# Routing steps of two mixture-of-experts layers moved to other places in a four-stage kernel

## The reference

```python
x = _layernorm(x + _L0_attn_ref(x, ...))   # gathered convolution, 8 heads, 32 taps
x = _layernorm(x + _L0_ffn_ref(x, ...))    # 8 experts, 2 chosen a token, GELU, hidden 512
x = _layernorm(x + _L1_attn_ref(x, ...))   # softmax attention, 16 heads of 8 channels
x = _layernorm(x + _L1_ffn_ref(x, ...))    # 8 experts, 2 chosen a token, gated SiLU, hidden 256
...
logits = xn @ gate_w_moe + gate_b_moe      # first FFN; the second has no bias and no inner norm
tw, ti = jax.lax.top_k(logits, K)
tw = jax.nn.softmax(tw, axis=-1)
```

## Time and profile before

| | us |
|---|---|
| three timed runs | 812.55, 816.96, 818.23; median 816.96 |
| the profiled execution, its own time | 811.2 |
| span from its first to its last instruction | 809.4 |

### The profile page before, as it was taken

The page is one execution under the profiler, slowest core; times in us unless marked ns, Lnnn a source line. Parts: engine busy times, 40 slices in busy tenths (PEclk is TensorE's granted clock), DMA queues, the critical chain, the costliest instruction groups (busy, mean ns, idle before and its releaser), DMA issues. The chain is left out here.

```text
span 809.4 us, 14477 instructions
## 1 busy us (share of the span) xinstructions
PE 530.4 (66%) x5186; PEld 439.2 (54%) x5186; DVE 531.9 (66%) x1210; ACT 413.3 (51%) x909; POOL 204.9 (25%) x195
## 2 busy tenths in 40 slices
PE   5367567575666379999832578888868803878730
PEld 4256566464566278899832444454544503878720
DVE  2989989999996225575624477888875304654734
ACT  5576766778852254477633436767654202333320
POOL 1111221222215312607045240000000070163444
PEclk9567868867777769999975668999985655999985
DMA  8354456554562301223111400000000011134322
GB/s 242 79 150 122 145 156 172 156 151 124 155 170 83 99 7 57 72 70 106 43 43 26 157 0 1 2 2 1 2 1 1 1 49 43 49 97 114 86 69 58
DMA packets 98891, 63.96 MB, mean 79 GB/s; under 512 B 57218, under 2 KB 89476, under 8 KB 98692
## 3 DMA queue, kind: packets, MB, share of 16 engines
q1 hardware_dynamic: 94564, 54.12, 23.3%
q0 software_dynamic: 4256, 8.92, 3.8%
HBM read 40.33 MB, written 22.68 MB: 78 GB/s over the span
## 5 line engine op out<-in xcount | busy, mean ns | idle before, releaser
L1866 DVE TENSOR_REDUCE mx<-s_ps 128x2 f32<-128x512 f32 x128 | 82.4, 687 | 28.3 <-PE s_ps L1627 28.2
L1803 ACT ACTIVATE pt<-st_ps 128x512 f32<-128x512 f32 x128 | 69.7, 600 | 36.2 <-PE st_ps L1637 35.4
L336 POOL DMA_INDIRECT xd<-xs_all,r_posA x32 | 33.4, 1044 | 201.2 <-DVE r_posA L320 192.1
L1269 ACT ACTIVATE hid<-up,wblk 128x128 f32<-128x128 f32 x184 | 52.9, 375 | 49.6 <-PE up L1168 49.6
L630 ACT ACTIVATE tap<-cst_s,par 128x328 f32<-128x328 f32 x128 | 72.3, 654 | 3.8 <-DVE par L994 3.8
L637 ACT ACTIVATE rest<-rest,par 128x264 f32<-128x264 f32 x128 | 53.7, 504 | 29.9 <-DVE rest L941 29.9
L618 POOL TENSOR_TENSOR kst<-kst 128x504 f32<-128x504 f32 x16 | 16.4, 1026 | 181.3 <-DVE kst L869 181.3
L1627 PE MATMUL s_ps<-kf,qf 32*128 32x256 f32 x256 | 34.7, 349 | 31.0 <-DVE mx L1866 25.8
L336 POOL DMA_INDIRECT xd<-xs_all,r_posB x32 | 33.9, 1059 | 76.0 <-DVE r_posB L320 66.9
L1168 PE MATMUL up<-xsT,wblk 128*128 128x128 f32 x368 | 52.2, 288 | 0.0
L2145 DVE COPY wblk<-wslab 128x768 f32 x46 | 26.8, 585 | 38.1 <-issue 23.6
(11 more groups left out here) (364 smaller groups left out, 1375.5 us busy)
## 6 DMA issues: line engine op xcount, KB each, us to landing
kd<-kst SPq DMA_DIRECT2D x16, 512.0 KB, 3.0
xc<-in_x_coarse SPq DMA_DIRECT2D x16, 512.0 KB, 4.2
yd<-eos SPq DMA_DIRECT2D x44, 128.0 KB, 1.9
xsb<-xd SPq DMA_DIRECT2D x20, 256.0 KB, 3.4
wslab<-in_w SPq DMA_DIRECT2D x8, 578.0 KB, 4.7
dW<-kd SPq DMA_DIRECT2D x16, 256.0 KB, 3.3
wslab<-in_w SPq DMA_DIRECT2D x1, 3072.0 KB, 10.4
xd<-zero_t SPq DMA_DIRECT2D x2, 1472.0 KB, 11.1
```

What stands on the lines that cost most here:

```text
L336: nc.gpsimd.indirect_dma_start(out=rows, out_offset=bass.IndirectOffsetOnAxis(ap=R.pos[:, t, k:k + 1], axis=0), in_=x[:, R.first + t, :], ...
L1269: nc.scalar.activation(hid[j % 2][:, k, :], up_ps[j % 2][:, k * P:(k + 1) * P], ACT.Gelu, bias=wblk[j % 4][:, 2 * DF + k:2 * DF + k + 1]). ...
L1803: nc.scalar.activation(pt[h % 8][:].rearrange("p t q -> p (t q)"), st_ps[k][:], ACT.Exp, scale=SCALE)\
L1866: nc.vector.tensor_reduce(mx[:, :, h:h + 1], s_ps[k][:].rearrange("p (t k) -> p t k", t=2), AX, ALU.max).then_inc(s_used, 1)
```

## The change

Four sets of lines move; no operation is dropped and apart from `half_rows_turned` (four of the eight transposes of `second_turned`) none is new.

- First attention: the steps of group A of the first FFN stand about one round earlier on PE, DVE and ACT. `route_owners` stays in round 14.
- First FFN: group B is normalised and turned completely before the first block; `route_logits` follows `up(0)`, `route_prefix` follows `down(0)`. On DVE the two `first_scales` stand ahead of the first `expert`, and the steps from `route_largest` to `route_slots` stand at j = 0 and 1 in place of j = 3 to 7.
- Second attention: group A of the second FFN is routed in rounds 6 and 7 (`i == B - 2`, `i == B - 1`), in `x_ps[2]`, with `route_owners` in round 8; before, rounds 8 and 9. PE waits for `cols_set` ahead of the maxima of round 7 and for `pos_set` ahead of those of round 8, since they write the same bank.
- Second FFN: `second_variances` stands ahead of the first `expert` on DVE, `second_turned` behind `up(1)` on PE, where it was the stage's first step, and the later steps of group B stand at j = 1 to 5 in place of j = 0 to 7.

The lines that go and come, with twelve columns of indentation taken off:

```diff
--- before.py
+++ after.py
@@ -235,6 +235,14 @@
+def half_rows_turned(nc, pe, R, x, bank, k, ident):
+    pe.wait_ge(R.rows_set, 1)
+    for t in range(4 * k, 4 * k + 4):
+        last = nc.tensor.transpose(bank[:, t % 4 * P:(t % 4 + 1) * P], x[:, R.first + t, :], ident[:])
+    last.then_inc(R.turned, 1)
@@ -679,29 +687,29 @@
     for n in range(NT):
-        if n == 12:
-            first_root(nc, act, R, 1)
         if n + 2 < NT:
             positions(n + 2)
+        if n == 10:
+            first_root(nc, act, R, 0)
         if n == 11:
...
             first_columns(nc, act, R, rows_ps, gb, 0)
+        if n == 12:
+            first_columns(nc, act, R, rows_ps, gb, 1)
         if n >= 2:
             mixed(n - 2)
-        if n == 12:
-            first_rows(nc, act, R, rows_ps, xs_all, 1)
         if n + 1 < NT:
...
         if n == 10:
-            first_root(nc, act, R, 0)
+            first_rows(nc, act, R, rows_ps, xs_all, 0)
+        if n == 11:
+            first_root(nc, act, R, 1)
         if n >= 2:
...
             transposed(n - 1)
-        if n == 10:
-            first_rows(nc, act, R, rows_ps, xs_all, 0)
-        if n == 12:
-            first_columns(nc, act, R, rows_ps, gb, 1)
+        if n == 11:
+            first_rows(nc, act, R, rows_ps, xs_all, 1)
     mixed(NT - 2)
@@ -747,15 +755,15 @@
             first_back(nc, pe, R, rows_ps, xs_all, 0, ident)
-        if (n, place) == (11, 2):
+        if (n, place) == (11, 1):
             pe.wait_ge(R.cols_set, 1)
             first_turned(nc, pe, R, rows_ps, sT, 1, ident)
+        if (n, place) == (12, 0):
+            first_back(nc, pe, R, rows_ps, xs_all, 1, ident)
         if (n, place) == (12, 2):
-            first_back(nc, pe, R, rows_ps, xs_all, 1, ident)
-        if (n, place) == (13, 0):
             pe.wait_ge(ld_ffn, 128)
             route_logits(nc, pe, R, rows_ps, gw)
-        if (n, place) == (14, 0):
+        if (n, place) == (13, 1):
             pe.wait_ge(zeroed, 1)
@@ -899,23 +907,24 @@
         R = routes[0]
+        if (n, place) == (9, 3):
+            first_variances(nc, v, link, R, rows_ps, 0)
         if (n, place) == (10, 0):
-            first_variances(nc, v, link, R, rows_ps, 0)
-        if (n, place) == (10, 2):
             first_scales(nc, v, link, R, 0)
+        if (n, place) == (11, 1):
+            first_variances(nc, v, link, R, rows_ps, 1)
         if (n, place) == (11, 3):
-            first_variances(nc, v, link, R, rows_ps, 1)
-        if (n, place) == (12, 0):
             first_scales(nc, v, link, R, 1)
-        if (n, place) == (13, 2):
+        if (n, place) == (12, 2):
             route_largest(nc, v, link, R, rows_ps, gbr)
-        if (n, place) == (13, 3):
+        if (n, place) == (12, 3):
             route_chosen(nc, link, R)
             route_counted(nc, v, link, R, it8)
-        if (n, place) == (14, 1):
+        if (n, place) == (13, 1):
             route_ends(nc, v, link, R, rows_ps)
-        if (n, place) == (14, 2):
+        if (n, place) == (13, 2):
             route_slots(nc, link, R, rows_ps)
+        if (n, place) == (14, 0):
             route_owners(nc, link, R, blk, WROW0)
@@ -1229,6 +1238,8 @@
 rows_turned(0)
+for k in range(2):
+    first_back(nc, pe, second, half[k], xs_all, k, ident)
 for j in range(TOTAL + 1):
@@ -1236,11 +1247,9 @@
         down(j - 1)
-    if j < 2:
-        first_back(nc, pe, second, half[j], xs_all, j, ident)
-    if j == 2:
+    if j == 0:
         route_logits(nc, pe, second, aux, gw)
-    if j == 6:
+    if j == 1:
         pe.wait_ge(zeroed, 1)
@@ -1310,18 +1319,18 @@
     first_root(nc, act, second, k)
-first_rows(nc, act, second, half[0], xs_all, 0)
+for k in range(2):
+    first_rows(nc, act, second, half[k], xs_all, k)
+rows_copied(0)
+for k in range(2):
+    first_columns(nc, act, second, half[k], gb, k)
 nc.scalar.activation(warm[:], eps_t[:], ACT.Gelu)
-rows_copied(0)
-first_rows(nc, act, second, half[1], xs_all, 1)
 route_share(nc, act, first)
...
             rows_copied(pair_of[j] + 1)
-    if 1 <= j < 3:
-        first_columns(nc, act, second, half[j - 1], gb, j - 1)
     if j == 5:
@@ -1442,11 +1451,10 @@
     first_variances(nc, v, link, second, half[k], k)
-for j in range(2):
-    expert(j)
 for k in range(2):
     first_scales(nc, v, link, second, k)
-expert(2)
+for j in range(3):
+    expert(j)
 for j in range(TOTAL + 1):
@@ -1454,19 +1462,17 @@
         route_shares(nc, v, first)
+    if j == 0:
+        route_largest(nc, v, link, second, aux, gbr)
+        route_chosen(nc, link, second)
+        route_counted(nc, v, link, second, it8)
+    if j == 1:
+        route_ends(nc, v, link, second, half[1])
+        route_slots(nc, link, second, half[1])
     if j == 3:
-        route_largest(nc, v, link, second, aux, gbr)
-    if j == 4:
-        route_chosen(nc, link, second)
-    if j == 5:
-        route_counted(nc, v, link, second, it8)
+        route_owners(nc, link, second, blk, WROW0)
     if j == 6:
         route_shares(nc, v, second)
-    if j == 7:
-        route_ends(nc, v, link, second, half[1])
-        route_slots(nc, link, second, half[1])
-    if j == 8:
-        route_owners(nc, link, second, blk, WROW0)
     if j in (11, 14, 17, 20):
@@ -1697,6 +1703,10 @@
         project(4 * i + 6)
+    if i == B - 1:
+        pe.wait_ge(routes[0].cols_set, 1)
+    if i == B:
+        pe.wait_ge(routes[0].pos_set, 1)
     if i - 1 in whole:
@@ -1711,6 +1721,9 @@
     values(i - 1, 0)
+    if i == B - 1:
+        pe.wait_ge(max_added, 2 * i)
+        half_rows_turned(nc, pe, routes[0], xs_all, x_ps[2], 1, ident)
     scores(i, 3)
@@ -1723,10 +1736,9 @@
         by_token(i - 2, 1, 1)
-    if i == B:
-        second_turned(nc, pe, routes[0], xs_all, s_ps, ident)
-    if i == B + 1:
-        route_prefix(nc, pe, routes[0], s_ps[1], tri)
+    if i == B - 1:
+        pe.wait_ge(ffn1_in, 32)
+        route_logits(nc, pe, routes[0], x_ps[2], wgs)
     scores(i, 4)
@@ -1749,9 +1761,10 @@
     scores(i, 6)
-    if i == B:
-        pe.wait_ge(ffn1_in, 32)
-        route_logits(nc, pe, routes[0], s_ps[0], wgs)
+    if i == B - 2:
+        half_rows_turned(nc, pe, routes[0], xs_all, x_ps[2], 0, ident)
+    if i == B - 1:
+        route_prefix(nc, pe, routes[0], x_ps[2], tri)
     if 4 * i + 9 < PROJ:
@@ -1823,13 +1836,13 @@
     powers(i - 1, 1)
-    if i == B:
-        second_root(nc, act, routes[0], 1)
     outputs(i - 2, 1)
...
     powers(i - 1, 4)
+    if i == B - 2:
+        second_root(nc, act, routes[0], 1)
     high(4 * i + 8)
@@ -1916,40 +1929,44 @@
     if i == B:
-        second_variances(nc, link, routes[0], xs_all)
-    if i == B + 1:
-        route_largest(nc, v, link, routes[0], s_ps[0], None)
-        route_chosen(nc, link, routes[0])
-        route_counted(nc, v, link, routes[0], it8)
+        route_owners(nc, link, routes[0], blk, WROW)
     largest(i, 1)
...
     add_maxima(i - 1, 1, 2)
-    if i == B:
-        second_rows(nc, v, link, routes[0], xs_all)
-        for k in range(2):
-            second_columns(nc, v, routes[0], s_ps, k)
     largest(i, 2)
     split(4 * i + 7)
+    if i == B - 2:
+        second_variances(nc, link, routes[0], xs_all)
     largest(i, 3)
+    if i == B - 1:
+        second_columns(nc, v, routes[0], (None, x_ps[2]), 1)
     if i == 0:
...
     averaged(i - 2)
-    if i == B + 1:
-        route_ends(nc, v, link, routes[0], s_ps[1])
-        route_slots(nc, link, routes[0], s_ps[1])
-        route_owners(nc, link, routes[0], blk, WROW)
+    if i == B - 1:
+        route_largest(nc, v, link, routes[0], x_ps[2], None)
     largest(i, 5)
+    if i == B - 2:
+        second_rows(nc, v, link, routes[0], xs_all)
+    if i == B - 1:
+        route_chosen(nc, link, routes[0])
+        route_counted(nc, v, link, routes[0], it8)
     split(4 * i + 8)
...
     negated(i, 1)
+    if i == B - 2:
+        second_columns(nc, v, routes[0], (x_ps[2],), 0)
+    if i == B - 1:
+        route_ends(nc, v, link, routes[0], x_ps[2])
+        route_slots(nc, link, routes[0], x_ps[2])
 projected(B - 1)
@@ -2063,18 +2080,19 @@
-second_turned(nc, pe, second, xs_all, rt_ps, ident)
 rows_turned(0)
...
         up(j)
+    if j == 1:
+        second_turned(nc, pe, second, xs_all, rt_ps, ident)
     if j >= 1:
         down(j - 1)
-    if j == 0:
+    if j == 1:
         route_logits(nc, pe, second, rt_ps[0], wgs)
-    if j == 4:
+    if j == 3:
         route_prefix(nc, pe, second, rt_ps[1], tri)
@@ -2159,32 +2177,32 @@
+second_variances(nc, link, second, xs_all)
 for j in range(3):
     expert(j)
-second_variances(nc, link, second, xs_all)
+second_rows(nc, v, link, second, xs_all)
 route_shares(nc, v, first)
-second_rows(nc, v, link, second, xs_all)
-for k in range(HALVES):
-    second_columns(nc, v, second, rt_ps, k)
 for j in range(TOTAL + 2):
...
         gated(j)
+    if j == 0:
+        for k in range(HALVES):
+            second_columns(nc, v, second, rt_ps, k)
     if j + 3 < TOTAL:
         expert(j + 3)
-    if j == 0:
```

(14 more changed lines are left out.)

## The result

The changed kernel took 768.56 us (median of four runs, 762.20 to 772.16) and the kernel before 815.92 beside it; the ratio is 0.941, with a 95% interval of 0.934 to 0.949. The profiled execution took 769.04 us, its span is 767.2.

A forecast was written before the change was run, and what follows sets the result against it. DVE bounds the first attention, PE the first FFN from block 9, PE and DVE in turn the second attention, then POOL's scatter alone. Gains 1.4 + 7 + 17.4 + 9 = 34.8 from 815.9 give 781 us; range 769 to 796.

The forecast's parts named there:

- Part 1: First attention: routing one round earlier lets POOL's scatter end before ACT; 1.4 us gained, bounds gain 1.7 and loss 3.
- the attention's own end stays: First attention: moved work adds nothing on DVE, so its end is unchanged unless a moved step waits; 0.3 us charged.
- Part 2: Opening of the first FFN: earlier scales and fewer stops before `up(7)`; 7 us gained, bounds 4 and 9.
- Part 3: Second attention: routing moved from rounds 8 and 9 to 6 and 7; 17.4 us gained, bounds 1.7 and 28.7.
- (a): End of the second attention: POOL's scatter leaves the path and the stage ends with its last addition; 19.7 us gained.
- (c): Second attention, rounds 6 and 7: they take on the routing; 10 us lost, between 1.0 and about 20.
- (b): Second attention, rounds 8 and 9: they lose the routing; 7.7 us gained, bounds 2 and 10.
- Part 4: Second FFN: `up(0)` no longer waits for group B's rows, PE's 5.28 wait goes; 9 us gained, bounds 4 and 11.
- (c) was 10.3, not 20: Rival: in rounds 6 and 7 engines wait so closely that the loss reaches 20 us; 791 us, chance 0.09.
- POOL's scatter ended before ACT, not at 280: Rival: all 16 scatter DMAs of the first attention are slowed beside DVE, ending at 280.6; 791 us, chance 0.05.
- positions came in time: Rival denied: second attention's positions come 12 us later than reckoned, so POOL still ends last; 798 us, chance 0.04.
- nearly all groups of A's blocks took 1.06: Rival denied: clock stays at 1.2 GHz in the first FFN's blocks, costing 1.84 each; up to 823 us, chance 0.04.

The follow-up runs named there:

- the first pair: First profiles of the changed kernel and of the kernel before: profiled executions of 769.04 and 811.2 us, a gain of 42 by the profiles.

## Why the prediction was wrong, point by point

**Part 1: 1.4 forecast, 7.7 measured (6.0 in the first pair).** The positions came as forecast (236.93 for 237.2). Beside DVE a DMA took 2.17 with its gap, nine of them, where 1.9 was forecast, so the scatter ended at 265.94, not near 264, but before ACT all the same. The Trainium skill (GPSIMD Engine Reference, section 8, Key points) has GpSimd contend with VectorE for its SBUF interfaces. The trace agrees on the mean: without its gap a DMA took 1.87 beside DVE and 0.96 without it, though three of the nine took 0.96 to 1.05.

Two steps failed. The first: "The stage then ends 271.99 - 270.25 = 1.74 earlier" kept the 2.64 behind POOL as if it stood behind any engine; behind ACT it is 0.69, so 1.95 was missing. The trace of before had a row that says so. At the end of the first FFN ACT ends last, at 454.00, and the next stage begins 0.55 behind it (0.54 to 0.56 in all 16 profiles):

```profile
453.41 0.59 ACT L1309 COPY sT<-aux 128x512 f32<-128x512 f32 x1 [2.57 <-PE aux L1226]
...
454.55 0.77 PE L1597 MATMUL x_ps<-xTh,wqkh 128*128 128x512 f32 x1 [1.17 <-PEq L1044]
```

The second: "the attention's own end stays". ACT ended 3.8 earlier on the mean, 2.5 of it behind DVE's last operation, where the transposes of the last tiles run faster; the last 16 of before and of the changed kernel:

```profile
259.69 3.22 PE L780 MATMUL tp_all<-ident,summed 128*128 128x128 f32 x16
```
```profile
258.56 1.97 PE L788 MATMUL tp_all<-ident,summed 128*128 128x128 f32 x16
```

I had asked of the prefix only whether it comes in time, not what 4.0 us of it at a clock of 0.50 do to the tiles behind it. The other 1.4 lie in DVE's own end (257.9 on the mean with the old order, 256.5 with the new); that is not explained, and the kernel with the prefix back has it too. The 0.3 charged for ACT did not show.

**Part 2: 7 forecast, 7.6 measured (6.55 in the pair, 6.9 over all executions).** Right, by other shares. In the pair `up(0)` gained 3.4 (2.4 forecast, though the forecast's own terms, 279.5 + 3.02 + 0.6 + 0.7, make 283.8 and not 284.3). From there to `up(7)` it gained 4.7 (6.2), as the logits took 3.42 and not 2.6, at half clock.

**Part 3: 17.4 forecast, 21.8 measured.** (a) was exact, 19.65 to 19.70 in the five profiles of before's kind. (c) was 10 and measured 10.3 (48.1 for 37.9), by 3.1 in round 6 (4.1 forecast) and 7.2 in round 7 (6.0). By the Trainium skill (ScalarE: Activation LUTs, What ACT_TABLE_LOAD costs) a drain comes on top of each table load. The trace of the changed kernel does not agree: both loads and the root between them took 577.13 - 574.31 = 2.82 us in round 6, so the 1.28 of the row was the right price.

```profile
574.31 1.28 ACT L212 ACT_TABLE_LOAD   x1
575.61 0.21 ACT L212 ACTIVATE r_vvA<-r_vvA 128x8 f32<-128x8 f32 x1
575.84 1.28 ACT L1816 ACT_TABLE_LOAD   x1
577.13 1.09 ACT L1816 ACTIVATE pt<-st_ps 128x512 f32<-128x512 f32 x2
```

(b), 7.7, was right for the longer form of rounds 8 and 9 (35.2 - 27.6 = 7.6) and far off for the shorter (13.0); the mean is 10.3, beyond its bound of 10. So (b) is the term of part 3 that was too small, and why rounds 8 and 9 come in two lengths stays open. The failed step of part 1 comes back at the stage's end: "2 to 3 us" from the last addition to the loads was 0.28 in the longer form. In the shorter form it was 0.93 and 0.97: there POOL's scatter had ended only 1.3 before the addition, and the loads came 2.22 and 2.23 behind POOL, so POOL still decides when that stage begins. On the mean this gives 1.6; the last 0.5 lie in the other rounds.

**Part 4: 9 forecast, 10.7 measured (9.6 in the pair).** Right step by step: `up(0)` at +5.4 (5 to 6), positions at +23.2 (23.6), PE at B's first rows at +49.4 (50.2).

**Rivals and range.** None of the four came: (c) was 10.3, not 20; POOL's scatter ended before ACT, not at 280; positions came in time; nearly all groups of A's blocks took 1.06 from 288.6 on. The miss of 13 us on the means is 6.3 + 0.6 + 4.4 + 1.7. One failed step, used twice, is the price of a barrier (about 1.9 and 1.6). The tail of the first attention gives 2.5 and rounds 8 and 9 give 2.6; both go with faster work on PE, and for neither is its cause settled. The other 4.4 are many small ones, the largest 1.7 of part 4 and 1.4 of DVE's own end. The range's low end set parts 2 and 4 and (c) at their best and left part 1 at 1.4 and (b) at 7.7; with the barrier priced by each engine's own distance it would have reached 765.

## What to carry to other kernels

Price a barrier for each engine by its own end and its own distance, and take the latest: an engine with a long distance can decide it without ending last. If work leaves POOL's end, what is gained is its overhang and at most the difference of the two distances, and the same trace may have a barrier of the other kind to read it from, as here. Ask of every group of narrow matmuls that is moved not only what waits for it, but at which clock the work behind it runs. And read a stage's spread from several executions before 2 us of a forecast are hung on one of them.

## What the runs showed of the hardware that was not expected

- The next stage began 0.28 us (first load) behind DVE, 0.54 to 0.56 and 0.69 behind ACT (first FFN, first attention), but 2.05 behind a memset and 2.63 to 2.66 behind an indirect DMA on POOL (2.22 to 2.24 to the first load in the second attention), and it did so even where POOL's DMA had ended 1.8 us before ACT.
- The granted clock was 0.58 in a stretch of 30.45 us in which PE was busy 27.18, with the narrow matmuls of rounds 8 and 9 and nine wide ones.
- The same program took 22.2 or 27.6 us in the same two rounds, with DVE's, ACT's and POOL's work equal to 0.05 us.
